# Four buffers for x's parts, an own stack for the first tile's LoRA rows, warm-up matmuls on a constant of zeros, and a small early read of the weights

## The reference, cut to what matters

```python
# layer 1 (per tile b): W 512x512, adapter A (512x16), B (16x512) picked by an index
base_out = einsum('bti,oi->bto', x, W) + b
lora_h = einsum('bti,bir->btr', x, A); lora_out = einsum('btr,bro->bto', lora_h, Bm)
h = base_out + lora_out * 2.0
# layer 2: base_w 512x512, A 64x512, router_w 16x512, experts B 16x512x64
base_out = h @ base_w.T + base_b
res_hidden = h @ A.T                        # 64 columns
probs = softmax(h @ router_w.T)             # 16 columns; top two, normalised
delta = einsum('bse,bsr,eor->bso', combine, res_hidden, B)
out = x + base_out + delta * 0.5
```

## Time and profile before

| | |
|---|---|
| time, median of 3 runs | 103.99 us |
| time of the profiled execution | 103.44 us |
| its span, first to last instruction | 101.6 us |
| PE busy | 97.4 us, 96% of the span |
| PEld (weight loads, overlapping PE) busy | 88.1 us, 87% |
| DVE, ACT, POOL busy | 65.1, 39.8, 18.7 us |
| mean granted TensorE clock | 0.999 of full speed |

### The profile page before, as it was taken

One profiled execution on the slowest core, in us unless ns is written; L12 is line 12 of the kernel. 1 busy time (PEld: TensorE's weight loads), 2 busy tenths in 40 slices (PEclk: granted clock), 3 DMA queues, 4 the chain that ended last, 5 costly groups with the idle time before them and its releaser, 6 DMA issues.

```text
span 101.6 us, 1806 instructions
## 1 busy us (share of the span) xinstructions
PE 97.4 (96%) x576; PEld 88.1 (87%) x576; DVE 65.1 (64%) x182; ACT 39.8 (39%) x97; POOL 18.7 (18%) x34
## 2 busy tenths in 40 slices
PE   5899999999999999999999999999999999999990
PEld 5799999999989999988988997899788788888990
DVE  2529999948567867959946735677368726656101
ACT  3404446885519726554435126120920604031000
POOL 5100003000397990070330061000000000000000
PEclk9999999999999999999999999999999999999999
DMA  2999789999854172592672280470065191940311
GB/s 42 321 318 377 225 182 372 340 424 422 230 96 68 26 216 58 168 267 68 182 254 59 79 231 1 117 205 6 14 165 165 20 266 46 239 170 0 110 52 52
DMA packets 8089, 16.91 MB, mean 166 GB/s; under 512 B 1475, under 2 KB 3907, under 8 KB 7952
## 3 DMA queue, kind: packets, MB, share of 16 engines
q1 hardware_dynamic: 7472, 16.40, 53.5%
q10 hardware_dynamic: 576, 0.39, 1.2%
q0 software_dynamic: 32, 0.00, 0.0%
HBM read 13.28 MB, written 2.16 MB: 152 GB/s over the span
## 4 chain that ended last, share of the span: by engine, by line
PE 71%; issue 11%; POOL 11%; DMA 3%; ACT 1%; DVE 0%; POOLq 0%
PE pair L771 69%; POOL x_lo L352 4%; POOL e_lo L370 4%; DMA w_raw_all<-w_cat 3%; POOL p_lo L364 2%; POOL p_hi L362 1%; PE pair L919 1%; PE pair L921 1%; ACT p_hi L418 1%; PE pair L939 1%; ACT w_hi_all L392 0%; DVE xn L765 0%; POOLq L361 0%
## 5 line engine op out<-in xcount | busy, mean ns | idle before, releaser
L771 PE MATMUL pair<-e_hi,w_hi_all 128*128 128x512 f32 (+1 forms) x72 | 27.2, 378 | 0.0
L771 PE MATMUL pair<-e_lo,w_hi_all 128*128 128x512 f32 (+1 forms) x72 | 26.7, 370 | 0.0
L771 PE MATMUL pair<-e_hi,w_lo_all 128*128 128x512 f32 (+1 forms) x72 | 26.6, 370 | 0.0
L771 PE MATMUL pair<-p_hi,x_hi 128*128 128x304 f32 x64 | 19.7, 308 | 0.2 <-POOL p_lo L364 0.2
L771 PE MATMUL pair<-p_lo,x_hi 128*128 128x304 f32 x64 | 19.4, 302 | 0.0
L771 PE MATMUL pair<-p_hi,x_lo 128*128 128x304 f32 x64 | 19.3, 302 | 0.0
L771 PEld LDWEIGHTS pair<-e_hi,w_lo_all 128*128 128x128 f32 x72 | 13.6, 188 | 2.6
L771 PEld LDWEIGHTS pair<-e_hi,w_hi_all 128*128 128x128 f32 x72 | 13.6, 188 | 2.4
L771 PEld LDWEIGHTS pair<-e_lo,w_hi_all 128*128 128x128 f32 x72 | 13.6, 189 | 1.8
L712 DVE TENSOR_TENSOR exp_raw_all<-w_raw_all 128x512 f32<-128x512 f32 x16 | 10.4, 689 | 7.5 <-DMA w_raw_all<-spill 7.5
L502 ACT ACTIVATE w_hi_all<-exp_raw_all 128x512 fp32r<-128x512 f32 x16 | 9.6, 627 | 13.8 <-DVE exp_raw_all L712 13.8
(11 more groups left out here) (107 smaller groups left out, 131.5 us busy)
## 6 DMA issues: line engine op xcount, KB each, us to landing
w_raw_all<-spill SPq DMA_DIRECT2D x16, 256.0 KB, 3.9
exp_raw_all<-experts SPq DMA_DIRECT2D x4, 512.0 KB, 8.7
xn<-x_n SPq DMA_DIRECT2D x4, 512.0 KB, 7.3
out<-xn SPq DMA_DIRECT2D x7, 256.0 KB, 4.0
w_raw_all<-w_cat SPq DMA_DIRECT2D x3, 552.0 KB, 6.8
xt_raw<-x_t SPq DMA_DIRECT2D x2, 512.0 KB, 6.3
xt_raw<-x_t SPq DMA_DIRECT2D x1, 1024.0 KB, 12.6
c_stack<-c_hi SPq DMA_DIRECT2D x7, 74.0 KB, 4.2
```

Of the source, the lines that this page charges most:

```text
L771: return nc.tensor.matmul(out_ap, lhs, rhs, start=first, stop=last)
```

## The change

It has six parts.

1. x's parts get four buffers: tiles 2 and 3 (and 6 and 7) use the first 512 columns of blocks 2 and 3 of `w_hi` and `w_lo`, free once the fold is done. ACT makes `x_hi` of tiles 2 and 3 right behind the folded parts, POOL their `x_lo` right behind the first adapters; for t from 4 on POOL makes the adapter's parts ahead of `x_lo`.
2. Tile 0's LoRA rows get an own stack of 98 partitions (`c_first`, `h_first`, `ht_first`): high parts at rows 0 and 32, low part at 64, bias at 96. Its product is two matmuls instead of eight. DVE fills parts of the stack with two copies, ACT with one; DVE now computes the low part of h before the transpose.
3. The warm-up matmuls read the constant of zeros that the program sets up by itself (`idle`, type F32, one column read again and again) instead of `e_hi` (type fp32r), wait for nothing, and are 13 instead of 11. Compiled, the program of before has 576 matmul instructions and 576 weight loads, as many as its source has matmuls; the changed one has 585 of each where its source has 572 matmuls: ahead of the fold stand 26 weight loads and 26 matmuls, two for each of the 13 (one with the high, one with the low part of the weights). 
4. POOL's queue reads 64 bytes of every eighth row of `w_cat` blocks 1 to 3 into `probe`, ahead of the slots; nothing uses them, and SP waits for them only at the end.
5. `b1` and `b2` are loaded behind the adapters' tables, `b2` into row 0 of a zeroed `b2_rows`, so the bias row costs no DVE step of its own.
6. ACT's first high part is made in two pieces of 128 columns; PE waits for the experts' last low parts only at the chunks that use them; some DVE and ACT work changes places (`c_hi` ahead of `bp_hi`, experts' splits later).

The core of the diff:

```diff
 T_H = P - 2 * R
+F_AGAIN, F_LOW, F_BIAS = 32, 64, 96
+FT = F_BIAS + 2
 NB = 3
+XB = 4
...
-WARM_UP = 11
+WARM_UP = 13
...
-        zeros = e_hi[:, 0, 0:2 * P]
+
+        idle = nc.const_aps.tensor(0.0, (P, 2 * P), F32)
...
+        def x_split(split, w_split):
+            return [split[:, b] for b in range(2)] + [
+                w_split[:, b, 0:D].rearrange("p (k n) -> p k n", k=KC) for b in range(2, XB)]
+
+        x_his, x_los = x_split(x_hi, w_hi), x_split(x_lo, w_lo)
...
-            sp.dma_start(b1_col[:, :], b1).then_inc(in_b, 16)
-            sp.dma_start(b2_row[:, :], b2).then_inc(in_b, 16)
...
+            pool.dma_start(probe[:, :, :], w_cat[1:KC, 0:P:8, 0:R].rearrange("k p n -> p k n")).then_inc(in_probe, 16)
             pool.dma_start(slot_row[:, :], slots).then_inc(in_slots, 16)
...
             x_lo_part(2)
+            x_lo_part(3)
             lora_a_parts(2)
             split_experts_lo(2)
-            x_lo_part(3)
             lora_a_parts(3)
             split_experts_lo(3)
             for t in range(4, NT):
+                lora_a_parts(t)
                 x_lo_part(t)
-                lora_a_parts(t)
...
-            nc.vector.memset(zeros.bitcast(F32), 0.0).then_inc(warm, 1)
+            nc.vector.memset(b2_rows[:, :], 0.0).then_inc(first_set, 1)
+            nc.vector.memset(c_first.bitcast(F32), 0.0).then_inc(first_set, 1)
+            nc.vector.memset(h_first[:, :], 0.0).then_inc(first_set, 1)
...
-            pe.wait_ge(warm, 1)
             for _ in range(WARM_UP):
-                last = mm(ps_warm, zeros[:, 0:P], zeros, True, True)
-            last.then_inc(pe_warm, 1)
+                mm(ps_warm, idle[:, 0:P], idle, True, True)
...
                 pe.wait_ge(ht_done, 1)
-                pe.wait_ge(ch_done, 1)
-                part(ht_first_hi[:, :], c_hi, False)
-                pe.wait_ge(cl_done, 1)
-                part(ht_first_hi[:, :], c_lo, False)
-                pe.wait_ge(ht_first_done, 1)
-                part(ht_first_lo[:, :], c_hi, False)
+                pe.wait_ge(first_high, 2)
+                pe.wait_ge(first_low, 1)
                 pe.wait_ge(bias_rows, 1)
-                part(ones[HR:HT, :], c_stack[HR:HT, 1, :], True).then_inc(pe_z, 1)
+                nc.tensor.matmul(ps_z[0][:, z_small[0]:BANK], ht_first[:, :], c_first[:, 0:border],
+                                 start=False, stop=True, skip_group_check=True)
+                nc.tensor.matmul(ps_z[0][:, BANK:BANK + W2N - border], ht_first[:, :], c_first[:, border:],
+                                 start=False, stop=True, skip_group_check=True).then_inc(pe_z, 1)
...
-                if t == 1:
-                    pe.wait_ge(bias_rows, 1)
-                else:
-                    pe.wait_ge(stacked_bias, 16)
+                pe.wait_ge(stacked_bias, 16)
```

More of the change, by code:

```diff
@@ L79, in adaln_ffn_kernel @@
         b1_col = sb("b1_col", [P, KC])
-        b2_row = sb("b2_row", [1, D])
+        probe = sb("probe", [P // 8, KC - 1, R])
+        b2_rows = sb("b2_rows", [P, W2N])
         w_hi_all = sb("w_hi_all", [P, KC * (D + W2N)], F32R)
@@ L141, in adaln_ffn_kernel @@
         ps_ht = pairs[3][0:2 * R, 0:P]
-        ps_ht_first = pairs[3][:, 0:P]
+        ps_ht_first = pairs[3][0:FT, 0:P]
         ps_rt = pairs[3][:, P:2 * P]
@@ L201, in adaln_ffn_kernel @@
         el_done = sem("el_done")
-        warm = sem("warm")
-        pe_warm = sem("pe_warm")
         consts = sem("consts")
-        low_row_set = sem("low_row_set")
+        first_set = sem("first_set")
+        first_high = sem("first_high")
+        first_low = sem("first_low")
         xh_done = sem("xh_done")
@@ L346, in _ @@
             pool.memset(probs[:, E:E + 8], -1.0).then_inc(consts, 1)
-            pool.memset(h_first[:, :], 0.0).then_inc(consts, 1)
             def x_lo_part(t):
-                par = t % 2
                 pool.wait_ge(xh_done, t + 1)
-                pool.tensor_tensor(x_lo[:, par].rearrange("p k n -> p (k n)"), xt_raw[:, t, :],
-                                   x_hi[:, par].rearrange("p k n -> p (k n)").bitcast(F32),
+                if t < XB:
+                    pool.wait_ge(pe_p, KC)
+                pool.tensor_tensor(x_los[t % XB], xt_raw[:, t, :].rearrange("p (k n) -> p k n", k=KC),
+                                   x_his[t % XB].bitcast(F32),
                                    ALU.subtract).then_inc(x_done, 1)
@@ L391, in _ @@
             act.wait_ge(in_w_side[0], 16)
-            nc.scalar.activation(w_hi[:, 0, W_LEFT], w_raw[:, 0, W_LEFT], ACT.Copy).then_inc(wh_left, 1)
+            for cols in (slice(0, P), slice(P, 2 * P)):
+                nc.scalar.activation(w_hi[:, 0, cols], w_raw[:, 0, cols], ACT.Copy).then_inc(wh_left, 1)
             act.wait_ge(in_w_side[1], 16)
@@ L583, in x_lo_early @@
                 dve.wait_ge(xh_done, t + 1)
-                nc.vector.tensor_tensor(x_lo[:, t].rearrange("p k n -> p (k n)"), xt_raw[:, t, :],
-                                        x_hi[:, t].rearrange("p k n -> p (k n)").bitcast(F32),
+                nc.vector.tensor_tensor(x_los[t], xt_raw[:, t, :].rearrange("p (k n) -> p k n", k=KC),
+                                        x_his[t].bitcast(F32),
                                         ALU.subtract).then_inc(xl_early, 1)
@@ L859, in x_side @@
                         pe.wait_ge(pl_done, KC)
-                    for n, (lhs, rhs) in enumerate(((x_hi, p_hi), (x_hi, p_lo), (x_lo, p_hi))):
-                        last = mm(ps_z[par][:, out_cols], lhs[:, par, k, :], rhs[:, k, cols],
+                    for n, (lhs, rhs) in enumerate(((x_h, p_hi), (x_h, p_lo), (x_l, p_hi))):
+                        last = mm(ps_z[par][:, out_cols], lhs[:, k, :], rhs[:, k, cols],
                                   k == 0 and n == 0, k == KC - 1 and n == 2)
@@ L946, in experts_product @@
                         pe.wait_ge(gl_done, 2 * t + (1 if c == 0 else 2))
+                    if t == 0 and c in (GH, GH + 2):
+                        pe.wait_ge(el_pool_done, (c - GH) // 2 + 1)
                     for n, (lhs, rhs) in enumerate(((gt_hi, e_hi), (gt_hi, e_lo), (gt_lo, e_hi))):
```

149 lines of the change are left out of this document (77 added, 72 removed).

## The result

The changed kernel takes 107.83 us, median of five runs (107.69 to 108.78), against 103.72 us for five runs of before (103.49 to 104.66). The ratio is 1.041, 95% interval 1.034 to 1.048: slower, by 4.1 us. The profiled execution takes 107.82 us, its span is 105.9 us.

The account below looks back on a forecast made before the run. PE was taken as the bound, a full conveyor from 4.24 to 99.09 us. Terms +4.15 - 1.09 + 0.10 - 0.34 = +2.8 us on 103.44 (median 103.99) us gave 106.5 us; range 105.0 to 108.2.

Parts of the forecast that it names:

- Warm-up: PE's start: 13 F32 warm-ups, compiled to 26 matmuls, move the fold from 4.24 to 9.2 us; +4.15 us.
- rivals 1 and 2: Warm-up: F32 matmuls run one column a step, no change, chance 0.06; or cost as before, 0.25 us each, faster, 0.08.
- if the clock rises as long after PE's start as before: Warm-up: upper clock level from 5.53 us, 4.68 us after PE's start; at 4.2 us +3.5, at 6.9 us +4.8.
- rival 1: Warm-up: F32 matmuls run at one column a step, fold at 6.4 us, total 103.4 to 104.6 us; chance 0.06.
- Tile 0's LoRA product: PE at 27.17 to 28.54 us: eight matmuls, 1.37 us, become two, 0.28 us; -1.09 us.
- Four waits ahead of it: Ahead of tile 0's LoRA product: PE waits for DVE's bias rows, done at 27.20 us; +0.1 us, up to 0.4.
- Four buffers: Tile 4's first product: POOL's earlier x_lo closes PE's gap there; -0.34 us, worst case it stays.
- stacked_bias: Tile 1's product waits for a DMA issued at 27.2 us; 0, with 0.4 us as the upper bound.
- Start of the loads: Tables, biases and next x come 1 to 3 us later behind the probe; hidden by the later fold, so 0.
- Rival 3: At 27 to 42 us the chain moves to a DMA or DVE; about 107.5 us, chance 0.03.
- more than 1 us in all: Behind the fold's start: the prediction is wrong if PE then waits for more than 1 us in all.
- full conveyor: PE from 4.24 to 99.09 us: continuously busy; after the change, fold's first matmul to PE's last 92.6 us.

Follow-up runs that it names:

- e4: The kernel before with only its warm-up changed to 13 matmuls on the F32 constant, no wait for the memset: 106.69 us, ratio 1.027 to before.
- e1: The changed kernel without the small read of the weights on POOL's queue: 107.52 us, ratio 1.034 to before.
- e2: The changed kernel with the warm-up constant read as fp32r, the small read kept: 108.89 us, no ratio given.
- e9: e6 with DVE's bias parts moved earlier, between the folded low parts: 103.26 us, ratio 0.990 to before.
- e5: e3 with POOL making x_lo of tiles 2 and 3 only after DVE's bias parts: 104.61 us, ratio 1.004 to before.
- e6: e3 with ACT's high part of the experts' quarter 2 ahead of tile 1's LoRA rows: 104.01 us, ratio 0.998 to before.
- e11: The changed kernel, F32 warm-up and read kept, with the experts' quarter 2 and DVE's bias parts moved earlier: 107.03 us, ratio 1.030 to before.
- e3: The changed kernel with the warm-up constant read as fp32r and without the small read: 105.13 us, ratio 1.013 to before.
- e10: e9 with the F32 constant again, but 4 warm-up matmuls instead of 13: 102.88 us, ratio 0.985 to before.

## Why the prediction was right, and where it was not

Direction, range and the main mechanism held: 107.83 us lies within 105.0 to 108.2, and e4 shows the warm-up alone as +3.0 us. The central number, 106.5 us, was 1.3 us low, and that the result lies in the range owes something to luck. Two errors had opposite signs: with the warm-up at the forecast +4.15 us instead of the measured +3.23, the same waits would have made it about 108.7 us, outside the range. The step that failed is the one on waits behind the fold's start: the sum has +0.1 us for them, measured are 2.2 us (0.94 and 1.25).

*Warm-up, "+4.15 us".* Measured +3.23. The price of a warm-up was right: I took 0.90 and 0.47 us for one warm-up, measured are 0.85 and 0.44. The factor 2 for an F32 operand, taken from one transpose, held, and rivals 1 and 2 are out; that a transpose is a fair stand-in for such a product no run shows, so it held by luck as much as by reasoning. What missed is "if the clock rises as long after PE's start as before": it rose 3.6 us after it, not 4.7. With the level changing at 4.4 us instead of 5.53 my own prices give 0.78 + 4 x 0.90 + 9 x 0.47 = 8.6 us for the fold's start instead of 9.2; the slightly high prices are the rest, down to 8.11. Against that the fold's first two matmuls cost 0.19 us more than their spacing (8.11 to 8.57); why, no run shows. In e4 the level changed 3.3 us after PE's start, in e1 5.1 us. My bounds, 4.2 to 6.9 us, did hold it. The Trainium skill, page "FP8 and Floating Point Precision", section "TensorE Precision Notes", says four passes for true FP32. The trace agrees, since an fp32r matmul of 256 columns starts 0.21 us after the last in e2 and an F32 warm-up takes 0.85 us at the same level. The prediction put rival 1 some 2.6 us below its sum; by its own terms (+4.15 against +1.3) it is 2.85.

*Tile 0's LoRA product, "-1.09 us".* Measured -1.02.

*Four waits ahead of it, "+0.1 us", at most 0.4.* The wait at the product was 0.36 us, within the bound. But PE had already lost 0.58 us ahead of it, at the transpose and behind the bias rows, which I had not listed as places where it could wait for DVE. This step failed. I took DVE's finish from the trace of before, 27.20 us, as if DVE's instructions kept their length and their place. They did not: the two bias parts grew by 1.4 us beside POOL's `x_lo`, which the change had moved to exactly there, and one bias part more, 0.9 us, stood behind DVE's last `p_lo`.

*Four buffers, "-0.34 us".* The gap at tile 4 went, as said; it was worth 0.44 us. The sentence behind it, that POOL "has x_lo of tiles 2 and 3 behind it long before", was true and incomplete: I asked only when POOL is done, not what runs on DVE meanwhile. The same omission for `e_lo` cost the largest single wait, 0.97 us with 0.28 us ahead of it, at a place for which the sum had no term. The trace of before already showed the price. DVE's `e_lo` took 1.22 us with POOL idle, and 1.53 us where POOL's `e_lo` (28.89 to 31.30 us) was still running:

```profile
23.82 1.22 DVE L611 TENSOR_TENSOR e_lo<-exp_raw_all,e_hi 128x1024 fp32r<-128x1024 f32 x1
...
30.86 1.53 DVE L611 TENSOR_TENSOR e_lo<-exp_raw_all,e_hi 128x1024 fp32r<-128x1024 f32 x1
```

The Trainium skill, page "VectorE: DVE Perf Modes", section "Two Vector instructions with no wait between them", names a second SBUF read interface that is shared with GpSimd. An instruction with two SBUF tensor inputs reads its second one through it, one in a 2-port perf mode its first. The section is about hangs and says nothing of waiting times. The rows agree with the first half: `bias_part` and `e_lo` have two and grow, `p_lo` reads one from PSUM and keeps its length beside POOL (in e9 two take 1.45 us, starting 0.42 us ahead of POOL's `x_lo`). The copy that grew in e5 has one SBUF input; which mode it ran in no run shows. That the interface is the cause is not shown by a run of its own. That lying side by side is, e6 shows for `e_lo`; for the bias parts e5 shows it for their length, and e9 and e11 for PE's waits only together with the new order.

*stacked_bias, "0, with 0.4 as the upper bound".* The product waited 0.28 us in the changed kernel's profile. In e1 and e3 it did not, and about as much (0.30 us) was lost instead at the next transpose, which needs what DVE computes behind `e_lo`. So it seems to have cost nothing of its own, as the sum has it.

*Start of the loads, "later by 1 to 3 us", cost 0.* ACT reached block 1 3.5 us later (11.08 against 7.59 us), and with the fold starting 1.1 us earlier than I had put it the cover was short by 0.20 us. That without the long warm-up the cover is gone is what e2 shows, but far dearer than the delay alone.

*Rival 3* put the chain on DMA or DVE at 27 to 42 us, 107.5 us, with a chance of 0.03. Its DVE half is what happened beside the forecast. It got so little because I argued against it with "the queues are emptier": this speaks against the DMA half only, and e3 shows that an earlier or later fold is no help to DVE, whose work moves along with PE's. The prediction's own mark, "more than 1 us in all" of waits, reads 0.9 us in the waits view and 2.4 us by the distances from start to start. I should have said by which; by distances it says that the prediction's picture of a full conveyor failed. The distance from the fold's first matmul to PE's last, forecast at 92.6 us, says the same: it is 95.2 us (8.11 to 103.29).

*What stays open*: why the clock rose at different times in kernels with the same warm-up, why PE's halt in e2 brought the lower level back in three runs of four, the arrival of block 1, which ACT starts on between 7.03 us (e10) and 8.04 us (e4), and how the 0.94 us of waits ahead of tile 0's product divide between collision and order.

## What to carry to other kernels

When a change moves work of DVE or GpSimd, list what the other of the two does in that stretch, not only who waits for the moved work. A warm-up is a number of matmuls times a price that depends on operand type; count it in the compiled program, and end it when the first data arrive. When a cover such as a long warm-up is removed, look at every late load that it had hidden before crediting the gain: here the shorter warm-up brought DVE's last addition 4.2 us forward without the read (e1 to e3), and 0.8 us back with it (after to e2, in the profile in which the lower clock level returned).

## What the hardware showed unexpectedly

- DVE beside a GpSimd `tensor_tensor` that started first: `bias_part` 0.83 us alone, 3.13 us for two; `e_lo` 1.22 us alone, 3.23 us; a 16x592 copy in SBUF 0.46 us alone, 1.37 us. GpSimd loses too where DVE is first: its cast 0.24 us alone, 1.24 us; `p_lo` 0.32 us alone, 1.35 us in e11; `x_lo` 1.28 us alone, 3.10 us for two that alternate with the bias parts. DVE's `p_lo`, with one operand in PSUM, keeps its length.
- A small read of 64-byte rows ahead of the slots on GpSimd's queue made their landing 5.3 to 6.6 us long (after, e2, e11) instead of 3.2 to 3.5. Behind them it did no harm (3.6 us), and it sped nothing up.
- After 2.65 us in which PE stood still the granted clock was 0.56 for 3.8 us, beginning 1.2 us after PE had resumed, in a profile where it had been 1.00 up to there. In the first 4 us of the changed kernel the spacing is that of the lower level (0.43 us) while the clock's record says 1.00.
- The same F32 warm-up reached the upper level 3.3, 3.6 and 5.1 us after PE's start in three kernels (e4, after, e1).
